# A Mamba scan kernel: scans and their inputs taken two blocks at a time, with the decay factors moved from PSUM to SBUF

## The reference

```python
xc, z = split(x @ W_in.T);  u = silu(causal_conv4(xc) + b_c)
dt, B, C = split(u @ W_x.T, [32, 48])
delta = softplus(dt @ W_dt.T + b_dt);  A = -exp(A_log)
# for every channel d and state n, over time t:
h[t, d, n] = exp(delta[t, d] * A[d, n]) * h[t-1, d, n] + delta[t, d] * u[t, d] * B[t, n]
y[t, d] = sum_n h[t, d, n] * C[t, n] + u[t, d] * D[d]
out = (y * silu(z)) @ W_out.T
```

## Time and profile before

| what | value |
|---|---|
| time of three runs | 9131.1, 9133.13, 9133.52 us (median 9133.13) |
| span of the profiled execution | 9119.7 us |
| busy: DVE / PE / POOL / ACT | 8449.9 / 7422.6 / 6002.9 / 5597.6 us |
| mean granted clock of TensorE | 0.937 of full speed |
| DMA | 61 GB/s on average |

### The profile page before, as it was taken

How to read it: one execution, slowest core, us unless ns; L and a number is a source line. 1 busy time by engine, 2 the same in 40 slices (tenths; PEclk the granted TensorE clock), 3 DMA queues, 4 the chain that set the end, 5 groups by cost and what they waited for, 6 DMA issues and landing times. The chain is left out here.

```text
span 9119.7 us, 124311 instructions
## 1 busy us (share of the span) xinstructions
PE 7422.6 (81%) x29640; PEld 3968.2 (44%) x29640; DVE 8449.9 (93%) x9986; ACT 5597.6 (61%) x9722; POOL 6002.9 (66%) x4680
## 2 busy tenths in 40 slices
PE   5788888888888888888888888888888888867886
PEld 3444444444444444444444444444444444444753
DVE  2999999999999999999999999999999999996716
ACT  5666666666666666666666666666666666643515
POOL 0777777777777777777777777777777777772203
PEclk7899999999999999999999999999999999968888
DMA  5111111111111111111111111111111111113434
GB/s 191 43 48 47 47 41 48 48 48 44 48 48 47 46 47 43 46 59 58 57 45 48 48 48 47 47 47 44 49 48 49 45 49 49 44 41 119 184 118 147
DMA packets 221783, 552.86 MB, mean 61 GB/s; under 512 B 24496, under 2 KB 24752, under 8 KB 200048
## 3 DMA queue, kind: packets, MB, share of 16 engines
q1 hardware_dynamic: 194672, 459.30, 15.8%
q10 hardware_dynamic: 26368, 84.95, 2.3%
HBM read 442.44 MB, written 101.71 MB: 60 GB/s over the span
## 5 line engine op out<-in xcount | busy, mean ns | idle before, releaser
L769 POOL TENSOR_TENSOR bu<-w,b_rep 128x512 f32<-128x512 f32 x4096 | 5210.2, 1276 | 2178.9 <-DVE h L804 2171.6
L804 DVE TENSOR_TENSOR_SCAN h<-decay,h_last,bu 128x512 f32<-128x512 f32 x3840 | 4882.7, 1272 | 28.5 <-POOL bu L769 19.9
L644 ACT ACTIVATE decay<-delta,neg_a 128x512 f32<-128x512 f32 x4096 | 2802.9, 689 | 2839.7 <-DVE h L804 2822.1
L438 PE MATMUL turn<-ident_m,h 128*128 128x128 f32 x16384 | 2698.5, 290 | 1321.7 <-DVE h L804 726.7
L438 PEld LDWEIGHTS turn<-ident_m,h 128*128 128x128 f32 x16384 | 1984.6, 147 | 3918.2 <-issue 2041.9
L815 DVE SCALAR_TENSOR_TENSOR acc<-turn,c_now,acc 128x512 f32<-128x512 f32 x3840 | 2777.3, 723 | 5.3 <-PE turn L438 4.0
L382 PE MATMUL proj<-x_conv,w_in 128*128 128x512 f32 x2048 | 1088.1, 624 | 54.7 <-issue 29.2
L382 PE MATMUL proj<-zy,w_out 128*128 128x512 f32 x2048 | 1050.0, 607 | 2.5 <-issue 2.5
L382 PE MATMUL proj<-conv_in,conv_diag 128*128 128x512 f32 x2048 | 1040.1, 602 | 9.6 <-ACT halo L561 9.6
L382 PE MATMUL proj<-x_gate,w_in 128*128 128x512 f32 x2048 | 1023.1, 594 | 0.0
L804 DVE TENSOR_TENSOR_SCAN h<-decay,zeros_m,bu 128x512 f32<-128x512 f32 x256 | 325.3, 1272 | 125.2 <-POOL bu L769 125.1
(11 more groups left out here) (167 smaller groups left out, 5480.4 us busy)
## 6 DMA issues: line engine op xcount, KB each, us to landing
b_rep<-b_rows SPq DMA_DIRECT2D x1024, 256.0 KB, 3.2
x_conv<-xt SPq DMA_DIRECT2D x32, 1024.0 KB, 6.2
x_gate<-xt SPq DMA_DIRECT2D x32, 1024.0 KB, 6.4
xt<-stage ACTq DMA_DIRECT2D x128, 256.0 KB, 2.4
x_n<-in_x_dram SPq DMA_DIRECT2D x16, 1024.0 KB, 5.2
xt<-xt_n ACTq DMA_DIRECT2D x16, 1024.0 KB, 4.1
x_l<-in_x_dram SPq DMA_DIRECT2D x16, 1024.0 KB, 5.7
mt_l<-xt SPq DMA_DIRECT2D x16, 1024.0 KB, 5.4
```

Source lines behind the costliest of these rows:

```text
L438: mm = pe.transpose(turn[:, tn.n % RING, b * P:(b + 1) * P], h[:, k % 2, b, j * P:(j + 1) * P], ident[:])
L644: act.activation(decay[:, b, :], delta[:, blk, :], ACT.Exp, scale=neg_a[:, n, blk:blk + 1]).then_inc(decay_set, 1)
L769: pool.tensor_tensor(bu[:, b, :], w[:, blk, :], b_rep[:, k % 4, :], ALU.mult).then_inc(bu_set, 1)
L804: dve.tensor_tensor_scan(h[:, k % 2, b, :], decay[:, b, :], bu[:, b, :], start, ALU.mult, ALU.add).then_inc(scanned, 1)
```

## The change

The work of a chunk is arranged anew; the mixture of experts and the input's layer norm stay as they are.

- **Scans of two blocks.** bu, decay and h get one more column per block. Two blocks lie side by side, and one scan instruction runs over 2 x 513 elements. Column 0 of decay is zero and column 0 of bu holds the start value, so the scan restarts there by itself. ACT copies that start value in (line 698). There are 64 scans a chunk where there were 128.
- **decay lies in SBUF** (`sb("decay", [P, 2, 2, 1 + T])`), not in PSUM. The banks go to turn (4) and to a ring for delta's projection (dproj, 2).
- **Inputs of two blocks.** One POOL instruction makes bu for two blocks (2 x 512 elements).
- **Five of sixteen states** (2, 5, 8, 11, 13; ten of the 32 groups) are scaled by C on ACT into prod (line 713), and POOL adds prod to acc, 1024 elements at a time (line 880). DVE leaves out these 40 of 128 tiles.
- **The skip term on PE:** u times a diagonal matrix of D is written to a turn bank, and ACT copies it to acc as the first summand (eight tiles a chunk). sum_y goes, and gate_y reads turn in PSUM and zy in SBUF.
- **Softplus:** the bias comes in as one more row of w_dt; ACT computes abs, exp and ln block by block, DVE finishes delta from PSUM and SBUF (line 950), POOL makes only w. ACT loads the table for exp and ln right behind each silu.
- **The timetable** is another: a table of the projections with earliest slots and lags.

The core of the diff:

```diff
+ORDER = [("conv_half", 0, 0), ("conv_half", 1, 0), ("delta", 4, 6), ("conv", 0, 8), ("conv_half", 2, 0), ("delta", 5, 0),
...
+BY_ACT = (2, 5, 8, 11, 13)
+SKIP_AT = (0, 15)
+TURNS = 4
...
-    ud = sb("ud", [P, NB, T])
...
-    bu = sb("bu", [P, 4, T])
-    h = sb("h", [P, 2, HB, T])
+    bu = sb("bu", [P, 2, 2, 1 + T])
+    decay = sb("decay", [P, 2, 2, 1 + T])
+    h = sb("h", [P, 2, HB, 1 + T])
+    prod = sb("prod", [P, J, HB * P])
-    stage = sb("stage", [P, 2, T])
+    stage = sb("stage", [P, T])
-    decay = ps("decay", [P, HB, T])
-    turn = ps("turn", [P, RING, T])
+    turn = ps("turn", [P, TURNS, T])
     proj = ps("proj", [P, RING, T])
+    dproj = ps("dproj", [P, RING, T])
...
+        def decay_of(G, kind, k, b):
             hf, n = divmod(k, STATES)
+            blk, s = hf * HB + b, HB * k + b
+            if b % 2 == 0:
+                act.wait_ge(scanned, G * SLOTS_BODY + (s - 2 + C_SCAN))
+                if kind.first or kind.enters:
+                    act.copy(bu[:, b // 2, :, 0], zeros[:, 0:2])
+                else:
+                    act.wait_ge(hlast_set, G * GROUPS + (k - GROUPS + 1 + C_HS))
+                    act.copy(bu[:, b // 2, :, 0], h_last[:, s:s + 2])
...
-            act.activation(decay[:, b, :], delta[:, blk, :], ACT.Exp,
+            act.activation(decay[:, b // 2, b % 2, 1:1 + T], delta[:, blk, :], ACT.Exp,
                            scale=neg_a[:, n, blk:blk + 1]).then_inc(decay_set, 1)
+        def product(G, kind, k, j):
+            act.wait_ge(turn_full, turn_base(G, kind) + (kind.turns.index[tile] + 1))
...
+            act.activation(prod[:, j, :], turn[:, kind.turns.index[tile] % TURNS, :], ACT.Copy,
+                           scale=c_now[:, j, k % STATES:k % STATES + 1]).then_inc(v_done, 1)
...
-            pool.wait_ge(scanned, G * SCANS + (4 * k + b + 1))
-            pool.tensor_tensor(bu[:, b, :], w[:, blk, :], b_rep[:, k % 4, :], ALU.mult).then_inc(bu_set, 1)
+            pool.wait_ge(scanned, G * SLOTS_BODY + (s - 2 + C_SCAN))
+            pool.tensor_tensor(bu[:, pr, :, 1:1 + T], w[:, blk:blk + 2, :],
+                               b_rep[:, k % 4, :].unsqueeze(1).to_broadcast([P, 2, T]), ALU.mult).then_inc(bu_set, 1)
+        def add_products(G, kind, k, jp):
+            lo = 2 * jp
+            pool.wait_ge(v_done, G * V_TILES + (kind.turns.by_act["state", k, lo + 1] + 1 + C_PROD))
+            pool.wait_ge(x_done, dve_base(G, kind) + (kind.turns.by_dve["state", k - 1, lo + 1] + 1 + C_TURN))
+            pool.tensor_tensor(acc[:, k // STATES, lo:lo + 2, :], acc[:, k // STATES, lo:lo + 2, :], prod[:, lo:lo + 2, :],
+                               ALU.add).then_inc(vsum_set, 1)
...
-            dve.tensor_tensor_scan(h[:, k % 2, b, :], decay[:, b, :], bu[:, b, :], start, ALU.mult, ALU.add).then_inc(scanned, 1)
+            dve.tensor_tensor_scan(h[:, k % 2, 2 * pr:2 * pr + 2, :].rearrange("p b t -> p (b t)"),
+                                   decay[:, pr, :, :].rearrange("p b t -> p (b t)"),
+                                   bu[:, pr, :, :].rearrange("p b t -> p (b t)"),
+                                   zeros[:, 0:1], ALU.mult, ALU.add).then_inc(scanned, 2)
...
+            elif k - 1 in ADDS:
+                dve.wait_ge(vsum_set, G * ADDS_ALL + (ADDS[k - 1] + j // 2 + 1 + C_PROD))
...
-            dve.tensor_tensor(zy[:, b, :], ud[:, b, :], zy[:, b, :], ALU.mult).then_inc(y_set, 1)
+            dve.tensor_tensor(zy[:, blk, :], turn[:, i % TURNS, :], zy[:, blk, :], ALU.mult).then_inc(x_done, 1)
```

More of the change, by code:

```diff
@@ L93, in timetable @@
[L93 to L104, removed]
+    at, end_of = 0.0, {}
@@ L128 @@
[L128 to L143, removed]
+            take[end + TAKE_LAG - TAPS_LEAD].append(("taps", x, i))
+        if kind in DELTA_KINDS:
+            for q, part in enumerate(("abs", "exp", "ln")):
+                take[end + TAKE_LAG + q].append((part + kind[5:], x, i))
+            delta_at[end + DELTA_LAG].append((kind, x, i))
+            w_at[(end + W_LAG) // 2].append((kind, x))
+        else:
+            take[end + TAKE_LAG].append((kind, x, i))
@@ new lines, in timetable, with tiles @@
+        if kind == "conv" and x % HB == HB - 1:
+            take[end + TAKE_LAG].append(("silu_u", x // HB, i))
+        if kind == "gate" and x % HB == HB - 1:
+            take[end + TAKE_LAG].append(("silu_z", x // HB, i))
+    return work, take, delta_at, w_at, end_of
+WORK, TAKE, DELTA_AT, W_AT, END_OF = timetable()
+def tiles(first, last):
+    place, acts, n, freed = {}, {}, 0, 0
+    for i, (kind, _, _) in enumerate(ORDER):
+        if first and kind in NOT_FIRST or last and kind in NOT_LAST:
+            continue
+        place[i], acts[i] = n, freed
+        n, freed = n + 1, freed + (kind not in DELTA_KINDS)
+    return place, acts, n, freed
@@ new lines, with by_act, __init__ @@
+TURN_AT = turn_tiles()
+CARRIED = [("state", GROUPS - 1, j) for j in range(J)] + [("y", 1, b) for b in range(HB)]
+def by_act(tile):
+    return tile[0] == "skip" or tile[0] == "state" and tile[1] % STATES in BY_ACT
+class Turns:
+    def __init__(self, order):
+        self.order = order
+        self.index = {t: i for i, t in enumerate(self.order)}
+        self.by_dve, self.by_act, dve, act = {}, {}, 0, 0
+        for t in self.order:
+            self.by_dve[t], self.by_act[t] = dve, act
+            if by_act(t):
+                act += 1
+            else:
+                dve += 1
+        self.n_dve, self.n_act = dve, act
@@ L154, in __init__, with has @@
         self.layer_next = layer + self.leaves
+        self.place, self.acts, self.n_tiles, self.n_freed = tiles(self.first, self.last)
+        self.turns = FIRST_TURNS if self.first else END_TURNS if over else ALL_TURNS
+    def has(self, what):
+        return not (self.first and what in NOT_FIRST or self.last and what in NOT_LAST)
 def all_chunks(eng, run):
@@ new lines, in turn_bank @@
+        def turn_bank(G, kind, tile):
+            i = kind.turns.index[tile]
+            if not kind.first or i >= TURNS:
+                turns, dve, act = kind.turns, dve_base(G, kind), G * V_TILES
+                if i < TURNS:
+                    turns, dve, act = ALL_TURNS, dve - ALL_TURNS.n_dve, act - V_TILES
+                user = turns.order[i - TURNS]
+                if by_act(user):
+                    pe.wait_ge(v_done, act + (turns.by_act[user] + 1 + C_PROD))
+                else:
+                    pe.wait_ge(x_done, dve + (turns.by_dve[user] + 1 + C_TURN))
+            return turn[:, i % TURNS, :]
@@ new lines, in turn_y, with turn_tile @@
+        def turn_y(out, summed, hf, b):
+            pe.wait_ge(x_done, summed)
+            for j in range(J):
+                mm = pe.transpose(out[:, j * P:(j + 1) * P], acc[:, hf, j, b * P:(b + 1) * P], ident[:])
+            mm.then_inc(turn_full, 1)
+        def turn_tile(G, kind, tile):
+            what, x, j = tile
+            out = turn_bank(G, kind, tile)
+            if what == "skip":
+                skip(out, G, kind.layer, x, j)
+            if what == "state":
+                turn_states(out, G - (tile in CARRIED), x, j)
+            if what == "y":
+                last = "state", x * STATES + STATES - 1, J - 1
+                turn_y(out, dve_base(G, kind) + (kind.turns.by_dve[last] + 1 + C_TURN), x, j)
@@ new lines, in copy_skip, with save_last @@
+        def copy_skip(G, kind, hf, j):
+            tile = "skip", hf, j
+            act.wait_ge(turn_full, turn_base(G, kind) + (kind.turns.index[tile] + 1))
+            act.copy(acc[:, hf, j, :], turn[:, kind.turns.index[tile] % TURNS, :]).then_inc(v_done, 1)
+        def save_last(G, k):
+            act.wait_ge(scanned, G * SLOTS_BODY + (HB * k + HB + C_SCAN))
+            act.copy(h_last[:, HB * k:HB * k + HB], h[:, k % 2, :, T]).then_inc(hlast_set, 1)
+        exp_tables()
+        X, n = 0, 0
@@ new lines, in _ @@
+        for b in range(HB):
+            w_of(0, b)
+        def body(G, kind):
+            for p in range(PAIRS):
+                if not kind.first:
+                    for what, x in W_AT[PAIRS + p]:
+                        w_of(G - 1 + (what == "delta_next"), x)
+                for what, x in W_AT[p]:
+                    if kind.has(what):
+                        w_of(G + (what == "delta_next"), x)
+                k, pr = divmod(p, 2)
+                inputs(G, k, pr)
+                if k - 2 in ADDS:
+                    add_products(G, kind, k - 2, pr)
@@ L872 @@
+        all_chunks(dve, body)
+        for tile in CARRIED:
+            if tile[0] == "state":
+                add_state(G_END, Kind(LAYERS - 1, over=True), tile[1], tile[2])
+            else:
+                gate_y(G_END, Kind(LAYERS - 1, over=True), tile)
 LOWEST = -3.4e38
```

726 lines of the change are left out of this document (371 added, 355 removed).

## The result

The changed kernel takes 12,520.35 us (median of four runs, 12,519.4 to 12,521.4) against 9133.33 for the kernel before on the same chip: 1.371 times as long, 95% interval 1.369 to 1.373. The forecast was 12,150 with a range of 10,600 to 13,100.

A forecast was written before the change was run, and what follows sets the result against it. DVE bounds the kernel before; in the changed one DVE and POOL exclude each other: 337 us held plus 8 of waits is 345 a chunk, times 32 plus 1110 outside gives 12,150 us, range 10,600 to 13,100.

The forecast's parts named there:

- The exclusion of scans and POOL's reading operations: In the chunks, a DVE scan with two SBUF streams and a POOL operation reading SBUF fully block each other; chance 0.74.
- The other signs named beforehand: In the changed trace: scans 4 to 4.7 us when waiting, inputs up to 4.6, additions unchanged at 0.72, clock below 0.96.
- The held time: Per chunk, scans hold the shared SBUF port 143 us, POOL's long operations 185 and w 9: together 337 us.
- The gaps: Waits between scans and POOL's operations, up to 15 us a chunk; 345 taken as the middle, 8 above 337.
- the upper end, 352: Longest chunk under the exclusion: 337 us held plus up to 15 us of waits and unhidden fixed parts.
- the handover after a scan: POOL's input starts on a semaphore after each scan: up to 64 x (0.08 + 0.15) = 15 us a chunk.
- All else under cover: DVE's other 67 us a chunk, ACT's 199 and PE's 215 lie beside the held port and cost nothing.
- the third rival: In the chunks, a lower clock makes PE's turns and products late, port idle meanwhile: 380 to 400 us a chunk; chance 0.05.
- The first rival: No exclusion for scans, engines run side by side: 228 us a chunk, 8406 us in all; chance 0.14.
- The sums of the engines: Work per chunk if engines ran freely: DVE 215 us, PE 215, POOL 206, ACT 199.
- The coupling: Without exclusion, close coupling of engines in a two-buffer ring lifts a chunk from 215 to 228 us, 13 more.
- The second rival: Scans wait for POOL but POOL not for scans: 299 us a chunk, 10,680 us in all; chance 0.06.

## Why the prediction was right, and where it was off

- **The exclusion of scans and POOL's reading operations.** Shown: by the stretched durations on both sides, by one tile moved to SBUF in the kernel before (309.1 us a chunk instead of 250.7), and by that tile moved back (no scan stretched). The other signs named beforehand came as well: scans up to 4.40, inputs up to 4.39, additions at their usual pace, a clock of 0.81. The chunk of 357.3 is just past the 335 to 355 that was named.
- **The held time, 337 us a chunk.** Right to about 1%: 340 us of the changed kernel's chunk have a scan or a POOL operation under way, and 338 with the later w. Inside it the double scan was mis-sized: 2.32 us alone, not 2.39. From 1.27 and 2.32 a scan has some 1.04 us per 512 elements and 0.23 fixed, not the 1.115 and 0.157 taken from another operation. 64 x 0.07 is 4.5 us that were counted too much, and fixed parts that are not hidden (up to 10 us were added above the 337 for them) stand against them, so the closeness of 337 is in part luck.
- **The gaps, 8 us a chunk on top.** This is the term that was too small: the chunk was 345 in the forecast and is 357.3, and 17.5 of it are idle of the port. Even the upper end, 352, was passed. Over 32 chunks that is 394 us; what lies outside the chunks took 1085 us and not 1110, which gives the 370 between 12,150 and 12,520. Only the handover after a scan had been counted. The prediction put POOL's w under what it holds (1.13 each) and not under what it waits for: delta, which DVE finishes behind a scan and two additions, while inputs stand queued behind w. Moving w later took 15 of the 17.5 us of idle away and made the chunk 17.1 us shorter, all of the 12 missing and more.
- **All else under cover.** DVE's additions, ACT's new work and PE cost little beside the port. DVE's scans do wait for decay (7 us a chunk) and for turns (5), but with the later w, at a granted clock of 0.82, such waits leave the port idle for 2.5 us a chunk at most. The clock came down to 0.81 and PE's busy time up to 235 us of 357; the third rival, late turns with the port idle meanwhile, would need far more idle than that.
- **The first rival (no exclusion) at 228 us a chunk.** Its condition was false, and its price was most likely too low. The sums of the engines (215, 215, 206, 199) are no estimate of a chunk in which they stand in rings of two buffers: with decay in PSUM it was 294, with POOL's inputs nearly gone 270 (the exclusion partly in force), with decay in PSUM and neither products nor early waits 272. The coupling had been put at 13 us; DVE's idle was 29 us in the shorter of the two with decay in PSUM. So it is doubtful that the change would have been faster than before even without the exclusion, but no run shows it: both kernels without exclusion have single scans and two turn banks where the change has double ones and four.
- **The second rival (half a lock)** is refuted by POOL's 4.34 and 4.36 above, and by tiny inputs of up to 2.26: POOL does wait for scans.

## What to carry to other kernels

Ask of every operation of VectorE whether both of its streams lie in SBUF, and whether GpSimd reads SBUF at the time; if so, the two engines are one resource there, and their times add up, as they did here for scans and for gate_y. Moving a tile from PSUM to SBUF to free banks can then cost more than the banks bring: in the kernel before it made a chunk of 251 us 58 us longer, and the changed kernel takes 357 us a chunk with decay in SBUF and four turn banks where it takes 294 with decay in PSUM and two. And do not take the sums of the engines for the chunk: where they are coupled through short rings, these kernels stood 29 us and more above them, though which part of the coupling costs it was not separated. An instruction that waits in an in-order queue holds up all that stands behind it, w before the inputs being the case here.

## What I had not expected of the hardware

A POOL memset and a two-stream scan run side by side at full speed (0.94 and 2.36 us), while a product of 2 x 8 elements waits up to 2.0 us for a scan. The blocked time is counted as the instruction's own. With one tile moved and the same instructions, DVE's busy time rose from 8449.9 to 10,195.1 us and POOL's from 6002.9 to 8718.9, so a high busy time does not say that an engine works.
